# Router logits of a fused attention and expert layer: one 4-byte matmul split into high and low halves in the rounded 4-byte type

## The reference

```
x = _layernorm(x + _L0_attn_ref(x, ...))
logits = x @ router_weight.T                  # 2048 x 512 times 512 x 64
topw, topi = jax.lax.top_k(softmax(logits), 8)  # then topw / sum(topw)
pos = (running count of the chosen expert) - 1  # capacity 256 per expert
xe[flat_e, pos] = x ; h = silu(g) * u ; y = sum over 8 of topw * down(h)
x = _layernorm(x + y)
```

## Time and profile before

| what | us |
|---|---|
| median of 3 runs | 2063.48 |
| lowest and highest run | 2063.23, 2065.95 |
| the profiled execution's own time | 2065.19 |
| its span, from the first instruction to the last | 2063.4 |
| busy time of TensorE matmuls in the span | 2037.8 |
| busy time of VectorE | 1670.6 |
| busy time of ScalarE | 1397.1 |
| busy time of GpSimd | 855.5 |

### The profile page before, as it was taken

How to read it: one execution, slowest core, us unless ns; L and a number is a source line. 1 busy time by engine, 2 the same in 40 slices (tenths; PEclk the granted TensorE clock), 3 DMA queues, 4 the chain that set the end, 5 groups by cost and what they waited for, 6 DMA issues and landing times.

```text
span 2063.4 us, 36116 instructions
## 1 busy us (share of the span) xinstructions
PE 2037.8 (99%) x11945; PEld 1745.4 (85%) x11945; DVE 1670.6 (81%) x3508; ACT 1397.1 (68%) x2726; POOL 855.5 (41%) x812
## 2 busy tenths in 40 slices
PE   9999999999999999999999999999989999999998
PEld 8888888888887888888888888788879999999996
DVE  6899997888778887788878887566678888898886
ACT  3677776766677666776666766433447777877776
POOL 1000023333233332333323333155557777788774
PEclk9999999999999999999999999999999999999999
DMA  7458564011340213401243010567649999999997
GB/s 267 184 219 294 222 234 147 21 72 49 125 144 21 72 56 125 137 21 72 81 167 131 25 69 26 203 244 286 242 152 261 298 296 295 303 296 295 296 285 265
DMA packets 130405, 361.07 MB, mean 175 GB/s; under 512 B 15312, under 2 KB 32208, under 8 KB 125648
## 3 DMA queue, kind: packets, MB, share of 16 engines
q1 hardware_dynamic: 102160, 292.03, 40.1%
q0 software_dynamic: 28096, 67.12, 13.6%
HBM read 224.21 MB, written 134.89 MB: 174 GB/s over the span
## 4 chain that ended last, share of the span: by engine, by line
PE 78%; DVE 4%; ACT 2%; POOL 1%; DMA 1%; issue 1%; POOLq 0%; DVEq 0%; ACTq 0%
PE p_S L724 18%; PE p_O L756 17%; PE p_TP L738 11%; PE p_pgu L1675 9%; PE p_acc L1144 8%; PE p_prest L1675 4%; PE p_py L1692 4%; PE p_tp L1660 3%; PE p_py L1693 1%; PE p_py L1694 1%; DVE p_nmax L879 1%; POOL p_odd L2149 1%; ACT p_prob L822 1%; PE p_lg L1166 1%; ACT p_pT1h L830 1%
## 5 line engine op out<-in xcount | busy, mean ns | idle before, releaser
L724 PE MATMUL p_S<-p_kT,p_q 128*128 128x512 f32 (+3 forms) x1920 | 458.5, 369 | 0.7
L724 PEld LDWEIGHTS p_S<-p_kT,p_q 128*128 128x128 f32 x1920 | 334.3, 188 | 62.8 <-ACT p_prob L822 10.7
L945 POOL TENSOR_SCALAR p_prob<-p_prob,p_inv 128x256 f32<-128x256 f32 (+7 forms) x256 | 193.3, 755 | 430.4 <-DVE p_inv L890 430.3
L945 POOL TENSOR_SCALAR p_prob<-p_prob,p_inv,p_part 128x1024 f32<-128x1024 f32 (+1 forms) x128 | 151.3, 1182 | 459.6 <-DVE p_inv L895 459.6
L879 DVE TENSOR_REDUCE p_nmax<-p_S 128x1 f32<-128x1024 f32 (+6 forms) x256 | 253.7, 991 | 97.3 <-PE p_S L724 92.9
L738 PE MATMUL p_TP<-p_ident,p_prob 128*128 128x128 f32 x2176 | 307.8, 273 | 5.8 <-DVE p_pT1l L900 3.1
L738 PEld LDWEIGHTS p_TP<-p_ident,p_prob 128*128 128x128 f32 x2176 | 248.9, 140 | 52.5 <-issue 22.1
L830 ACT CAST p_pT1h<-p_TP 128x512 fp32r<-128x512 f32 (+2 forms) x320 | 164.7, 551 | 107.5 <-PE p_TP L738 107.3
L830 ACT CAST p_pT0h<-p_TP 128x384 fp32r<-128x384 f32 (+3 forms) x320 | 147.7, 498 | 128.4 <-PE p_TP L738 128.2
L1943 POOL DMA_INDIRECT sum_scratch<-p_y,p_tokT x124 | 206.3, 1663 | 42.6 <-issue 36.9
L756 PE MATMUL p_O<-p_pT1h,p_v 128*128 128x512 f32 x584 | 222.5, 412 | 0.4 <-DVE p_pT1l L900 0.2
(11 more groups left out here) (356 smaller groups left out, 4547.0 us busy)
## 6 DMA issues: line engine op xcount, KB each, us to landing
p_w_raw<-in_gu SPq DMA_DIRECT2D x64, 768.0 KB, 6.8
qk_scratch<-p_qout SPq DMA_DIRECT2D x80, 512.0 KB, 2.8
p_q<-qk_scratch SPq DMA_DIRECT2D x16, 2048.0 KB, 9.3
o_scratch<-p_oT SPq DMA_DIRECT2D x64, 512.0 KB, 3.3
p_ot<-o_scratch SPq DMA_DIRECT2D x32, 1024.0 KB, 7.2
p_w_raw<-in_gu SPq DMA_DIRECT2D x64, 256.0 KB, 8.2
v_scratch<-p_vout SPq DMA_DIRECT2D x16, 512.0 KB, 2.9
p_t_raw<-in_dn SPq DMA_DIRECT2D x32, 256.0 KB, 8.4
```

Source lines behind the costliest of these rows:

```text
L724: mm = nc.tensor.matmul(out if k0 // 512 == (k1 - 1) // 512 else out.rearrange("p (n k) -> p n k", n=2), x, y, start=(n == 0), stop=(n == 2))
L945: nc.gpsimd.tensor_scalar(prob[k][:, cols], prob[k][:, cols], inv[:, k:k + 1], scale, ALU.mult, ALU.mult).then_inc(normed, 1)
```

## The change

Weights and rows of the router are split into halves of type `F32R`. `xtp` is copied to `x1_s[HI]` by ScalarE, and VectorE writes `x1_s[LO] = xtp - x1_s[HI]`, between `place(b-1)` and what follows it. `rw_s` holds both halves of the weights side by side, made once at the stage's start. Four products of 128 columns (high rows times both halves at once) and four of 64 columns (low rows times high weights) go to `lg`, now 128 columns wide. VectorE adds the two halves of `lg` into `logit` in SBUF, and the choice reads `logit`. `logits` is moved behind the ninth head of the block, `ROUTE` from 8 to 9. The last block keeps the float32 product. The semaphore `copied` is counted twice a block. Shortened diff:

```diff
+        x1_s = [sb(f"x1T{s}", [P, NC, P], F32R) for s in "hl"]
+        rw_s = sb("rwTs", [P, NC, 2, E], F32R)
+        logit = sb("logit", [P, E])
-        lg = ps("lg", [P, E])
+        lg = ps("lg", [P, 2 * E])
...
-            TABLE, TURN, ROUTE, SUM = 3, 6, 8, 14
+            TABLE, TURN, ROUTE, SUM = 3, 6, 9, 14
...
             def logits(b, early):
-                pe.wait_ge(copied, b + 1)
-                if not early:
+                pe.wait_ge(copied, b * 2 + 2)
+                if early:
+                    pe.wait_ge(lower_ready, 3)
+                else:
                     pe.wait_ge(topped, b)
                 for c in range(NC):
-                    mm = nc.tensor.matmul(lg[:], x1T[:, c, :], rwT[:, c, :], start=(c == 0), stop=(c == NC - 1))
+                    nc.tensor.matmul(lg[:], x1_s[HI][:, c, :], rw_s[:, c].rearrange("p s e -> p (s e)"), start=(c == 0),
+                                     stop=(c == NC - 1))
+                for c in range(NC):
+                    mm = nc.tensor.matmul(lg[:, 0:E], x1_s[LO][:, c, :], rw_s[:, c, HI, :], start=False, stop=True,
+                                          skip_group_check=True)
                 mm.then_inc(routed, 1)
+            def last_logits():
+                ...
+                for c in range(NC):
+                    mm = nc.tensor.matmul(lg[:, 0:E], x1T[:, c, :], rwT[:, c, :], start=(c == 0), stop=(c == NC - 1))
...
-                nc.scalar.copy(x1T[:], xtp[:]).then_inc(copied, 1)
+                nc.scalar.copy(x1T[:] if last else x1_s[HI][:], xtp[:]).then_inc(copied, 1)
...
+            nc.vector.tensor_copy(rw_s[:, :, HI, :], rwT[:]).then_inc(lower_ready, 1)
+            dve.wait_ge(lower_ready, 2)
+            nc.vector.tensor_tensor(rw_s[:, :, LO, :], rwT[:], rw_s[:, :, HI, :].bitcast(F32), ALU.subtract).then_inc(lower_ready, 1)
...
+            def rows_lo(b):
+                dve.wait_ge(copied, b * 2 + 1)
+                nc.vector.tensor_tensor(x1_s[LO][:], xtp[:], x1_s[HI][:].bitcast(F32), ALU.subtract).then_inc(copied, 1)
...
+                    link(nc.vector.tensor_reduce(logit[:], lg[:].rearrange("p (s e) -> p e s", s=2), AX_X, ALU.add))
+                    whole = logit[:]
-                link(nc.vector.max(top[:], lg[:]))
+                link(nc.vector.max(top[:], whole))
...
                     if not (first and k == 0):
                         place(b - 1, 1 - k, first)
+                    rows_lo(b)
                     if last:
                         weights_lo(dve, b)
                     choose(b, k, i, first)
```

More of the change, by code:

```diff
@@ L1016, in stage_route @@
         upper, lo, hi = sb("upper", [P, TOPK]), sb("lo", [P, TOPK]), sb("hi", [P, TOPK])
+        sb.end = -(-sb.end // 128) * 128
+        x1_s = [sb(f"x1T{s}", [P, NC, P], F32R) for s in "hl"]
+        rw_s = sb("rwTs", [P, NC, 2, E], F32R)
+        logit = sb("logit", [P, E])
         near, near_hot = sb("near", [P, QUICK]), sb("near_hot", [P, QUICK, CAP], F16)
@@ L1155, in turn @@
                 if not early:
-                    pe.wait_ge(copied, b)
+                    pe.wait_ge(copied, b * 2)
                 for c in range(NC):
@@ L1161, in logits @@
             def logits(b, early):
-                pe.wait_ge(copied, b + 1)
-                if not early:
+                pe.wait_ge(copied, b * 2 + 2)
+                if early:
+                    pe.wait_ge(lower_ready, 3)
+                else:
                     pe.wait_ge(topped, b)
                 for c in range(NC):
-                    mm = nc.tensor.matmul(lg[:], x1T[:, c, :], rwT[:, c, :], start=(c == 0), stop=(c == NC - 1))
+                    nc.tensor.matmul(lg[:], x1_s[HI][:, c, :], rw_s[:, c].rearrange("p s e -> p (s e)"), start=(c == 0),
[3 more added lines that the diff above has]
+                                          skip_group_check=True)
+                mm.then_inc(routed, 1)
+            def last_logits():
+                pe.wait_ge(copied, NB * 2 - 1)
+                pe.wait_ge(topped, NB - 1)
+                for c in range(NC):
+                    mm = nc.tensor.matmul(lg[:, 0:E], x1T[:, c, :], rwT[:, c, :], start=(c == 0), stop=(c == NC - 1))
                 mm.then_inc(routed, 1)
@@ L1209, in step @@
                         turn(b - 1, 1 - k, first)
-                    project(b, k, range(TURN, ROUTE), not after)
+                    project(b, k, range(TURN, H // 2), not after)
+                    pe.wait_ge(ot_in[k][1], i * 16 + 16)
+                    project(b, k, range(H // 2, ROUTE), not after)
                     if after:
                         logits(b - 1, first)
-                    pe.wait_ge(ot_in[k][1], i * 16 + 16)
                     project(b, k, range(ROUTE, SUM), not after)
@@ L1227, in tensor @@
             table(NB - 3)
-            logits(NB - 1, False)
+            last_logits()
             keep_busy(nc, 4, acc[0][:, 0:P], ident[:])
@@ L1249, in root, with copy @@
                 nc.scalar.activation(sd[:], mv[:, 1:2], ACT.Sqrt, bias=eps[:]).then_inc(sd_ready, 1)
-            def copy(b, early=False):
+            def copy(b, early=False, last=False):
                 act.wait_ge(turned, b + 1)
@@ L1289, in scalar @@
             root(NB - 1)
-            copy(NB - 1)
+            copy(NB - 1, last=True)
             exp(NB - 1)
@@ L1341, in best @@
                 wait_alone(dve, passed, routed, b + 1)
-                link(nc.vector.max(top[:], lg[:]))
-                link(nc.vector.match_replace(left[:], top[:], lg[:], LEAST))
-                nc.vector.tensor_tensor(mask[:], lg[:], left[:], ALU.is_gt).then_inc(masked, 1)
-                link(nc.vector.max_index(topi[:], top[:], lg[:]))
+                if isinstance(b, int) and b == NB - 1:
+                    whole = lg[:, 0:E]
+                else:
+                    link(nc.vector.tensor_reduce(logit[:], lg[:].rearrange("p (s e) -> p e s", s=2), AX_X, ALU.add))
+                    whole = logit[:]
+                link(nc.vector.max(top[:], whole))
+                link(nc.vector.match_replace(left[:], top[:], whole, LEAST))
+                nc.vector.tensor_tensor(mask[:], whole, left[:], ALU.is_gt).then_inc(masked, 1)
+                link(nc.vector.max_index(topi[:], top[:], whole))
                 nc.vector.tensor_scalar(ntop[:], top[:, 0:1], -1.0, None, ALU.mult).then_inc(topped, 1)
@@ L1362, in choose @@
             def choose(b, k, i, early):
-                link = chain(choose_step, 6, b)
+                link = chain(choose_step, 7, b)
                 best(b, k, i, early, link)
@@ L1472, in vector @@
             place(NB - 3, 1, False)
+            rows_lo(NB - 2)
             choose(NB - 2, 0, NB // 2 - 1, False)
```

## The result

The changed kernel takes 2080.4 us (median of 6 runs), the kernel before 2063.88 (median of 6). By the two medians it is 16.5 us slower; the ratio on record is 1.0076, with a 95% interval from 1.0066 to 1.0086, which is some 16 us too. The direction was forecast, the size was not: 6.9 us were, and the time lies outside the range. Its profiled execution took 2081.5, with a span of 2079.6, 16.2 above the span before.

The account below looks back on a forecast made before the run. TensorE bound the kernel at 13.04 a block; the change would make a 13.37 loop bind: 4.3 + 0.9 + 0.7 + 0.7 + 0.4 - 0.1 = 6.9 us slower, 2063.48 + 6.9 = 2070.4, range 2065.0 to 2073.0.

Parts of the forecast that it names:

- the 0.7 of the move: Logits behind the ninth head come 0.70 later; free while TensorE bounds, but the tail after block 14 starts 0.70 later.
- The bound changes from TensorE to the loop through ScalarE: Route stage: a turn through `hi_equal`, `hi_hot`, table load, square root and low half takes 13.37, against TensorE's 13.04.
- The products: TensorE's eight new router products per block were to take 0.84, like the old eight, leaving TensorE's own period at 13.04.
- the first rival: Router products get cheap, 0.05 a load; loop 12.99, TensorE 12.66; about +1.6, 2065.1; chance 0.08.
- nor are they dearer: Rival on TensorE's rounded products: 0.12 each, 0.15 on each of 13 turns and the last, +2, 2072.4; chance 0.12.
- The terms of the loop: Pieces of one turn, from the first weight load of one block's logits to the next's, summing to 13.37.
- the extra 0.15: In every second block `hi_hot` on ScalarE comes later, 0.15 over a period; 6 x 0.15 = 0.9.
- `max` to `hi_equal`: 3.33: Loop term on VectorE, from `max` in the choice to the comparison `hi_equal`: 3.33, read from the trace before.
- the prediction's own two additions: VectorE's new work per block: low half of the rows 0.68, sum of the logits' two halves 0.44.
- The split of the weights costs nothing: Start of the stage: two VectorE instructions of 256 elements fit while the residual sum waits for GpSimd until 1322.97.
- The blocks with expert weights: Blocks 12 and 13: the expert's weight split delays the choice by 0.36 more, 0.7 for both.
- The tail: After block 14's logits: 0.70 of the move and 0.44 of the sum, less 0.1 for a shorter stalled start.

Follow-up runs that it names:

- root_first: Changed kernel with GpSimd's residual sum behind the shares, ScalarE's square root ahead of the previous block's `hi_hot`, and table products behind the turn: 2068.55 us, ratio 1.0016.
- residual_behind_choice: Changed kernel with GpSimd's residual sum (`xb`) held back until VectorE has written the block's shares: 2070.5 us, ratio 1.0028.
- root_first_late_split: root_first with the split of the router weights moved from ahead of the first residual sum to behind the first normalisation: 2067.89 us, ratio 1.0012.
- route_8: Changed kernel with the logits back behind the eighth head: 2080.29 us, ratio 1.0076.

## Why the prediction was wrong

The 16.2 us between the two profiled spans stand in four stretches (the 0.7 of the move counted where it first shows):

| stretch | forecast, us | measured, us |
|---|---|---|
| up to the logits of block 1 | 0.7 | 1.7 |
| the 13 turns up to the logits of block 14 | 5.9 | 13.6 |
| from these to the last logits | 0.3 | 0.0 |
| from the last logits to the end | 0.0 | 0.9 |

- **The bound changes from TensorE to the loop through ScalarE: right.** The chain, the vanished idle time before the square root and the logits released by the low half are as foretold, and turning ScalarE's order round removes it.
- **The products: right.** 0.89 from the first load of the logits to the load behind them (1399.37 to 1400.26), as in the stalled block before (1522.24 to 1523.13), 1.01 in both where TensorE doesn't stop (1406.02 to 1407.03 before, 1407.32 to 1408.33 in root_first), and the old period in root_first. The cheap rounded products of the first rival don't exist; nor are they dearer.
- **The terms of the loop**, in the block without a collision: load to sum 1.24, sum 0.43, `max` to `hi_equal` 3.08 (3.33 forecast), to `hi_hot` 1.33 (1.25), to the table load 1.16, load 1.30, square root 0.33, to the low half 3.58, to the load 0.73. Together 13.18, where the prediction had 13.37 and 0.15 more in every second block. The 3.33 was read from a block in which the shares, at 0.38, were already longer than their 0.23, and the extra 0.15 didn't come back. Too much by some 3.4 us over 13 turns, which hid a part of the next miss.
- **The step that failed is "`max` to `hi_equal`: 3.33"**, carried over from a schedule in which the residual sum came behind the shares. The prediction named no neighbour of that stretch on GpSimd. In the new schedule it is 4.16 (1401.04 to 1405.20), 1.08 more than in the free block. The trace of before had the margin, 5.28 against 4.73 after `hi`, 0.55, and the prediction's own two additions behind `hi` put VectorE later by more. The two met in full in nine of the 13 turns and in part in one. That is the 10 us which residual_behind_choice gives back.
- **The split of the weights costs nothing: wrong.** Its cover was the wait for the residual sums, and beside just these its two instructions took 1.39 and 1.40 instead of the 0.29 and 0.43 that they take elsewhere. TensorE waited 0.96 for block 0. Moving it put the logits of block 1 0.47 earlier (root_first against root_first_late_split).
- **A term that the prediction left out**: in block 1 TensorE already waits 0.5 for the low half (13.14 from the logits of block 0 to its own instead of 12.63), in root_first and root_first_late_split too. With the 0.7 of the move and the 0.96 that is 2.2; the table has 1.7 because TensorE came to this stage 0.5 earlier in the profiled execution of the changed kernel.
- **The blocks with expert weights**: 13.79 and 13.87, 0.6 to 0.7 over 13.18, where 0.36 was forecast for each.
- **The tail**: the sum in block 14 was to add 0.44 less 0.1, but the last logits come 11.88 after those of block 14, before 11.90: there too the stretch from `max` to `hi_equal` is shorter (1527.32 to 1530.39, before 1511.71 to 1515.10) and pays for it. The 0.9 stand behind the last logits. Their eight float32 loads took 1.37 instead of the 0.97 of the earlier trace rows, at a granted clock of 0.80 of full speed between 1535 and 1540, a mean over its two levels, where before had full speed at these loads; `max` follows the first load by 1.71 instead of 1.26, which is 0.45. The other half can't be assigned: from the last logits to the end the profiled executions take from 539.6 (route_8) to 543.8 (residual_behind_choice).

```profile
1537.53 1.37 PEld L1183 LDWEIGHTS p_lg<-p_rwT,p_x1T 128*128 128x128 f32 x8 [0.40 <-ACT p_x1T L1274]
```

What is left open: root_first_late_split is 3.0 above before in the medians and 3.1 in the spans. Of the 3.1, 1.0 stands before the logits of block 1, 0.3 less than before in the turns, 0.3 more from block 14 to the last logits, and 2.1 behind these. There the granted clock was the lower of its two levels (0.50 of full speed between 1525 and 1530), and `tokT` came 7.65 after the first load of the last logits, where before needs 5.98. The profiled execution of root_first, with the same instructions in that place, had the full clock at these loads, also needs 5.98, and its span is 1.3 above before. So 1.7 of the 3.1 go with the clock. In the 5 us ahead of them TensorE's matmuls were busy for 2.7 in either, so what decided it no run shows.

## What to carry to other kernels

When a change adds work to an engine that "has idle time", walk the loop that goes through its in-order stream and its neighbours' once, and add it up against the bound; here 2.6 us of idle time hid a reserve of under one (the prediction's 13.37 less its two additions, 1.12, against 13.04). Then look at what runs on GpSimd beside each short VectorE instruction of that loop in the new order, not the old: one of 0.23 us took 1.3 in nine of 13 turns, because in a loop that bounds itself both kept their distance from the same `hi`. And count instructions of TensorE before expecting a gain from another number type: eight loads stayed eight.

## What the runs showed of the hardware

- A VectorE instruction of 8 numbers a row stands still for the remainder of a GpSimd sum that began 0.02 earlier (1.30; 0.75 with half the sum); the other way round the sum takes 2.11 instead of 1.30. I had seen the 2.11 in the trace before and not asked why.
- Which of the two goes first was decided by hundredths of a microsecond (5.40 against 5.42 after `hi`): the free block and its neighbours differ only in an input that came 2.28 late, and that late transfer saved a microsecond.
- Weight loads of the rounded type pace products of 128 and 64 columns just as those of float32 do: 0.89 for eight in both where TensorE had waited, 1.01 in both where it had not.
- The same collision costs 1.08 a block where the loop through VectorE is the bound and 0.13 to 0.18 where TensorE is.
